# Attention and feed-forward on one core: row halves that exchange two banks, and weighing in 64-row pieces

## What is computed

```python
xn = _layernorm(x, axis=-1)                       # 4 x 2048 x 256
# attention: q, k, v = xn @ W + b, 16 heads of 16, q and k with rotary positions
scores = jnp.einsum('bhnd,bhmd->bhnm', q, k) / jnp.sqrt(jnp.float32(d))
weights = jax.nn.softmax(scores, axis=-1)
inter = jnp.einsum('bhnm,bhmd->bhnd', weights, v)
attn = inter.transpose(0, 2, 1, 3).reshape(b, n, d) @ Wo + bo
# feed-forward: w = where(k, 1, -1)
h = s0 * (concatenate([xn, -xn]) @ w0)            # 512 -> 1024
h = relu(h) * 2;  h = s1 * (h @ w1);  h = relu(h) * 2   # 1024 -> 1024
y = x + attn + s2 * (h @ w2)                      # 1024 -> 256
```

## Time and profile before

| | us |
|---|---|
| median of 3 runs | 2763.39 |
| lowest and highest run | 2763.38, 2764.12 |
| the profiled execution | 2764.13 |
| its span in the profile | 2762.3 |
| PE busy | 2670.4 (97%) |
| ScalarE (ACT) busy | 2099.4 (76%) |
| VectorE (DVE) busy | 957.2 (35%) |
| GpSimd (POOL) busy | 301.8 (11%) |

### The profile page before, as it was taken

One profiled execution on the slowest core, in us unless ns is written; L12 is line 12 of the kernel. 1 busy time (PEld: TensorE's weight loads), 2 busy tenths in 40 slices (PEclk: granted clock), 3 DMA queues, 4 the chain that ended last, 5 costly groups with the idle time before them and its releaser, 6 DMA issues.

```text
span 2762.3 us, 49767 instructions
## 1 busy us (share of the span) xinstructions
PE 2670.4 (97%) x21063; PEld 1416.9 (51%) x21063; DVE 957.2 (35%) x1535; ACT 2099.4 (76%) x2301; POOL 301.8 (11%) x265
## 2 busy tenths in 40 slices
PE   7999499999999999999999999999999999999997
PEld 6777245454444445454545454544545454545444
DVE  6776222323232323242332333232423223232322
ACT  4556388888888887878787878788887878787883
POOL 4666100000000000000000000000000000000000
PEclk9999699999999999999999999999999999999998
DMA  8888412212222222122121222221222222222213
GB/s 252 256 260 251 109 40 55 55 51 55 59 59 59 74 54 72 52 71 69 48 71 55 70 66 74 57 78 50 75 57 59 64 60 67 60 74 66 73 25 111
DMA packets 288417, 228.67 MB, mean 83 GB/s; under 512 B 184129, under 2 KB 227905, under 8 KB 281665
## 3 DMA queue, kind: packets, MB, share of 16 engines
q1 hardware_dynamic: 279744, 217.08, 28.6%
q10 hardware_dynamic: 8448, 8.39, 0.9%
HBM read 140.46 MB, written 84.93 MB: 82 GB/s over the span
## 4 chain that ended last, share of the span: by engine, by line
PE 80%; ACT 5%; issue 2%; SPq 1%; DMA 1%; DVE 0%; POOLq 0%; POOL 0%; DVEq 0%
PE ps_o L946 33%; PE ps_f L981 23%; PE ps_s L931 21%; ACT probs L911 5%; PE ps_f L994 2%; PE ps_f L1036 0%; SPq L826 0%; DMA xT_lo<-xn_lo_d 0%; DMA probs<-rest_sum_d 0%; PE ps_o L1036 0%; DVE k_rows L1141 0%; SPq L823 0%; DMA heads_t<-heads 0%; SPq L728 0%; POOLq L740 0%
## 5 line engine op out<-in xcount | busy, mean ns | idle before, releaser
L911 ACT ACTIVATE probs<-ps_s 128x1024 f32<-128x1024 f32 x2048 | 1945.5, 1032 | 480.1 <-PE ps_s L931 469.4
L946 PE MATMUL ps_o<-probs,v_ones 128*32 128x512 f32 x8192 | 1011.3, 600 | 0.0
L931 PE MATMUL ps_s<-q_rows,k_rows 50*128 50x512 f32 x4096 | 858.7, 440 | 35.6 <-DMA q_rows<-row_shift 31.0
L931 PEld LDWEIGHTS ps_s<-q_rows,k_rows 50*128 50x128 f32 x4096 | 366.8, 184 | 688.0 <-ACT probs L911 600.7
L1110 DVE TENSOR_SCALAR h_hi<-ps_f 128x512 fp32r<-128x512 f32 x224 | 154.4, 689 | 921.5 <-PE ps_f L981 921.4
L946 PEld LDWEIGHTS ps_o<-probs,v_ones 128*32 128x32 f32 x8192 | 200.6, 108 | 426.6 <-issue 331.0
L981 PE MATMUL ps_f<-h_hi,ffn_w 64*128 64x512 f32 x2048 | 409.7, 395 | 0.0
L981 PE MATMUL ps_f<-h_lo,ffn_w 64*128 64x512 f32 x2048 | 405.2, 390 | 0.0
L1055 POOL TENSOR_TENSOR heads<-heads,sums 128x512 f32<-128x512 f32 x64 | 82.5, 1289 | 2166.9 <-DVE sums L1076 2166.9
L1076 DVE RECIPROCAL sums<-sums 128x128 f32<-128x128 f32 x256 | 228.4, 925 | 1.1
L981 PEld LDWEIGHTS ps_f<-h_hi,ffn_w 64*128 64x128 f32 x2048 | 196.3, 186 | 37.3 <-issue 10.1
(11 more groups left out here) (102 smaller groups left out, 1611.9 us busy)
## 6 DMA issues: line engine op xcount, KB each, us to landing
k_rows<-k_parts SPq DMA_DIRECT2D x128, 256.0 KB
q_rows<-q_parts SPq DMA_DIRECT2D x384, 64.0 KB
q_parts<-parts SPq DMA_DIRECT2D x32, 512.0 KB, 3.7
k_parts<-parts SPq DMA_DIRECT2D x32, 512.0 KB, 5.5
k_rows<-k_parts SPq DMA_DIRECT2D x128, 128.0 KB
x_chunk<-in_x ACTq DMA_DIRECT2D x16, 512.0 KB, 6.1
xn_hi_d<-xn_hi SPq DMA_DIRECT2D x16, 512.0 KB, 4.4
xn_lo_d<-xn_lo SPq DMA_DIRECT2D x16, 512.0 KB, 5.2
```

Of the source, the lines that this page charges most:

```text
L911: nc.scalar.activation(probs[:, s % PBUF, half * 2 * C:(half + 1) * 2 * C], ps_s[:, half].rearrange("p c n -> p (c n)"), ACT.Exp, scale=SC ...
L931: last = nc.tensor.matmul(ps_s[:, half, w], k_rows[rows, u, t * P:(t + 1) * P], q_rows[rows, u, half], start=True, stop=True)
L946: last = nc.tensor.matmul(ps_o[32 * c:32 * c + 2 * DH], v_ones[:, u, t], probs[:, s % PBUF, c * C:(c + 1) * C], start=(t == 0), stop=(t == ...
```

## The change

The feed-forward work goes in groups of two outputs with two stages. In stage 0 the upper row half adds to bank 0 and the lower to bank 1; in stage 1 they change banks (`bank = half ^ stage`), so that both halves of a sum meet in the bank itself. ps_f has two banks instead of three, and ps_o two instead of one. VectorE copies a finished group's two banks to raw, and makes hi and lo from there. carry goes. The third layer is one group: a bank holds two outputs of 256 columns.

Weighing issues, for each step, eight matmuls of 64 rows by 32 columns: four with the upper 64 keys into one bank of ps_o, four with the lower into the other. `finish` copies one bank and adds the other.

The parts are spread evenly: VISITS_PER_ROUND gives the three visits of a round 4, 2, 2 parts in the first layer, 3, 3, 2 in the second and 6, 5, 5 in the third, hence 4, 16 and 4 rounds. Before it is 4, 15 and 5. The projection moves from round 31 to 39, the pass's last, and SP's store of y to the end of the pass.

```diff
-BANKS = 3
+GROUPS = (FT // 2, FT // 2, 1)
-PROJECT_AT = 3 * len(BURSTS) + 1
+PROJECT_AT = 4 * len(BURSTS) - 1
+VISITS_PER_ROUND = ((4, 2, 2), (3, 3, 2), (6, 5, 5))
+K_LAST = FT - 2
+def stage_parts(layer):
+    if layer < THIRD:
+        return [(0, k, low) for k in range((DT, FT)[layer]) for low in range(2)]
+    return [(t, k, low) for ks in (range(K_LAST), range(K_LAST, FT)) for t in range(TT // 2) for k in ks for low in range(2)]
...
-        carry = sb("carry", [P, 2, C], F32)
+        raw = sb("raw", [P, 2, C], F32)
-        ps_o = ctx.enter_context(nc.psum_tensor("ps_o", [P, C], F32))
-        ps_f = ctx.enter_context(nc.psum_tensor("ps_f", [P, BANKS, C], F32))
+        ps_o = ctx.enter_context(nc.psum_tensor("ps_o", [P, 2, C], F32))
+        ps_f = ctx.enter_context(nc.psum_tensor("ps_f", [P, 2, C], F32))
...
-                sp.wait_ge(group_used, outs_before(i, projects) + OUTS[projects] + BANKS)
+                sp.wait_ge(group_used, 2 * number_of(i + 1, FIRST, 0))
+                if projects:
+                    sp.sem_inc(turn_begun, 1)
+                    sp.dma_start(y_out[b - 1, r], y[:]).then_inc(y_stored, 16)
                 sp.sem_inc(turn_begun, 1)
                 sp.dma_start(rest_out[b, r], rest[:]).then_inc(rest_stored, 16)
                 store_head(i, HEADS - 1)
...
-                for c in range(CB):
-                    last = nc.tensor.matmul(ps_o[32 * c:32 * c + 2 * DH], v_ones[:, u, t], probs[:, s % PBUF, c * C:(c + 1) * C],
-                                            start=(t == 0), stop=(t == KT - 1))
+                for half in range(2):
+                    rows = slice(GROUP_ROWS * half, GROUP_ROWS * (half + 1))
+                    for c in range(CB):
+                        last = nc.tensor.matmul(ps_o[32 * c:32 * c + 2 * DH, half], v_ones[rows, u, t],
+                                                probs[rows, s % PBUF, c * C:(c + 1) * C], start=(t == 0), stop=(t == KT - 1))
...
+                if first and stage == 1:
+                    pe.wait_ge(stage_done, number - max(0, i - CB) + 1)
+                if first and stage == 0:
...
+                    if number > 0:
+                        pe.wait_ge(group_used, 2 * number - 1)
...
                 for half in range(2):
+                    if half == 1 and first and stage == 0 and number > 0:
+                        pe.wait_ge(group_used, 2 * number)
                     rows = slice(GROUP_ROWS * half, GROUP_ROWS * (half + 1))
+                    bank = half ^ stage
...
+                number = number_of(i, THIRD, 1)
                 pe.wait_ge(y_loaded, 32 * i - 32 * (CB - 1))
                 for t in range(TT):
+                    half, n = t // 2, t % 2
+                    if n == 0:
+                        pe.wait_ge(group_used, 2 * number - 1 + half)
...
-                nc.vector.tensor_copy(heads[:, u], ps_o[:]).then_inc(raw_ready, 1)
+                nc.vector.tensor_copy(heads[:, u], ps_o[:, 0]).then_inc(half_kept, 1)
+                dve.wait_ge(half_kept, HEADS * i + j + 1)
+                nc.vector.tensor_tensor(heads[:, u], heads[:, u], ps_o[:, 1], ALU.add).then_inc(raw_ready, 1)
...
+                for bank in range(2):
+                    nc.vector.tensor_copy(raw[:, bank], ps_f[:, bank]).then_inc(group_used, 1)
...
             def take_projected(i):
...
-                for t in range(TT):
-                    at = PROJECT_PLACE + t
-                    dve.wait_ge(group_done, outs_before(i, True) + at + 1)
-                    nc.vector.tensor_tensor(y[:, t], ps_f[:, at % BANKS, 0:D], y[:, t], ALU.add).then_inc(group_used, 1)
+                dve.wait_ge(group_done, number_of(i, THIRD, 1) + 1)
+                for half in range(2):
+                    pair = y[:, TT // 2 * half:TT // 2 * (half + 1)].rearrange("p t d -> p (t d)")
+                    nc.vector.tensor_tensor(pair, ps_f[:, half], pair, ALU.add).then_inc(group_used, 1)
...
+                    for layer, group in ENDS[n]:
+                        take(i, layer, group)
                     if ended % KT == 0:
                         finish(i, j)
```

More of the change, by code:

```diff
@@ L105, in rounds @@
         out.append(left[:n])
-        ends.append([(layer, phase) for visit in left[:n] for layer, phase, part in visit if part == size_of(layer) - 1])
+        ends.append([(layer, group) for visit in left[:n] for layer, group, stage, *part in visit
+                     if stage == 1 and last_of(layer, stage, tuple(part))])
         left = left[n:]
@@ L979, in beside @@
-                    begins = part == 0 and (half == 0 or phase == 0)
-                    ends = part == size - 1 and (half == 1 or phase == sums_in(layer) - 1)
-                    last = nc.tensor.matmul(to, lhs, rhs, start=begins, stop=ends)
-                    if ends:
-                        last.then_inc(group_done, 1)
-                    elif part == size - 1:
-                        last.then_inc(half_done, 1)
+                    bank = half ^ stage
+                    if layer == THIRD:
+                        out = TT // 2 * bank + t
+                        to, lhs, rhs = ps_f[:, bank, t * D:(t + 1) * D], (h2_hi, h2_lo)[low][rows, k, out * P:(out + 1) * P], w2[rows, k]
+                    else:
+                        out = 2 * group + bank
+                        to, on = ps_f[:, bank], slice(out * P, (out + 1) * P)
+                        lhs = (w0, w1)[layer][rows, k, on]
+                        rhs = ((xT_hi, xT_lo), (h1_hi, h1_lo))[layer][low][rows, k]
@@ L1006, in one_pass @@
                         if 0 <= visit < len(VISITS[n]):
[L1007 to L1008 removed]
+                            for part in VISITS[n][visit]:
+                                beside(i, *part)
                     if projects and n == PROJECT_AT:
@@ L1076, in invert, with take @@
                 nc.vector.reciprocal(at, at).then_inc(sums_inverted, 1)
-            def keep(i, projects, layer):
-                bank = ps_f[:, place(projects, layer, 0) % BANKS]
-                dve.wait_ge(group_done, outs_before(i, projects) + place(projects, layer, 0) + 1)
+            def take(i, layer, group):
+                number = number_of(i, layer, group)
+                done = SUMS * i + FT * layer + 2 * group
+                dve.wait_ge(group_done, number + 1)
                 if layer == THIRD:
@@ new lines, in take @@
+                    for bank in range(2):
+                        to = rest[:, TT // 2 * bank:TT // 2 * (bank + 1)].rearrange("p t d -> p (t d)")
+                        nc.vector.scalar_tensor_tensor(out=to, in0=ps_f[:, bank], scalar=w["scale"][:, 0:1], in1=to,
+                                                       op0=ALU.mult, op1=ALU.add).then_inc(group_used, 1)
+                    return
+                if done > 0:
+                    dve.wait_ge(part_ready, done)
+                for bank in range(2):
+                    nc.vector.tensor_copy(raw[:, bank], ps_f[:, bank]).then_inc(group_used, 1)
```

143 lines of the change are left out of this document (47 added, 96 removed).

## The result

| | us |
|---|---|
| changed kernel, median of 4 runs | 2811.73 |
| lowest and highest run | 2809.08, 2812.81 |
| kernel before, median of 4 runs | 2763.39 |
| ratio, 95% interval | 1.0174, 1.0156 to 1.0191 |
| the profiled execution, its span | 2812.81, 2811.0 |

The change makes the kernel 48 us slower. The forecast was 20 us slower.

What follows compares the result with a forecast made beforehand. PE, at 97% of the span, was taken as the bound. Terms of -32.6, +2.0, +38.5, +2.0 and +10.4 gave +20.3 us on a span of 2762.3, so 2784 us as median, range 2762 to 2813.

Steps and rivals of the forecast that it cites:

- visits, 16 passes: Feed-forward rounds in each pass: evenly spread parts save 2.04 us a pass, -32.6 us; first-layer rounds taken at 4.97.
- pieces of 64 rows, 16 passes: Weighing: eight pieces side by side start the last one 0.027 us later in each two-step round, +10.4 us.
- projecting passes, 12: Round after the projection: 12 projecting passes lose the 0.17 us they had from an idle ScalarE, +2.0 us.
- wait at the boundary, 11: Start of the pass after passes 4 to 14: first feed-forward pair waits 3.5 us for VectorE's y adds, +38.5 us.
- half clock at it, 11: Pass boundaries: rival that PE's idle 2.6 us lowers the clock, +28 us, 2812; 12%, not in the sum.
- end: Last pass: the additional add and the y adds stand before the final reciprocals, +2.0 us, up to +5.
- The rival that it is hidden: Pass boundary: the next pass's first part does not wait for VectorE, so the time is 2746; 4%.
- the rival in series: Weighing: the eight pieces do not run together, each round ends 0.43 us later, +275 us, 3059; 8%.
- That ScalarE covers it in one-step rounds: Weighing in one-step rounds: ScalarE's 0.14 us covers the 0.027 us delay, so only two-step rounds count it.
- VectorE's: VectorE's added copies and adds: some 200 us more busy time on an engine at 35%, priced 0.
- The switch: Change between scores and weighing: columns still change, so the 0.10 us pause stays, 0 us; rival of a free switch, 2653, 7%.

Runs made afterwards that it cites:

- kernel 5: Changed kernel with VectorE adding the projection into y before finishing head 3, and weighing in 128 rows by 32 columns without VectorE's add: 2743.04 us.
- kernel 2: Changed kernel with 13 extra score pairs, results overwritten, issued by PE before the wait at the start of passes that follow a projecting one: 2790.86 us.
- kernel 4: Kernel before with only its feed-forward visits spread evenly (16 second-layer and 4 third-layer rounds) and the projection one round later: 2757.43 us.
- Kernel 1: Changed kernel with two VectorE calls exchanged: in a pass's last round it adds the projection into y before finishing head 3, not after: 2754.72 us.
- kernels 6 and 7: Changed kernel, y additions before head 3's end, weighing one query chunk in 128 columns: two 64-row pieces, 2617.16 us, or one 128-row piece, 2768.02 us.
- kernel 3: Changed kernel with weighing as before, four matmuls of 128 rows by 32 columns into one bank, and VectorE's copy without the add: 2786.73 us.

## Why the prediction was off

The terms beside what the runs measure, in us:

```
term                                  forecast   measured   from
visits, 16 passes                      -32.6      -25.9     147.37 -> 145.75 (kernel 5)
pieces of 64 rows, 16 passes           +10.4      +10.2     145.75 -> 146.39 (kernel 5, changed)
projecting passes, 12                   +2.0       +2.5     +3.45 -> +3.66 on a pass
wait at the boundary, 11               +38.5      +39.4     5.085 -> 8.67 (kernel 2)
half clock at it, 11                     0        +20.4     8.67 -> 10.53 (changed)
end                                     +2.0       +1.4     pass 15 to the end, 186.0 -> 192.1, less the above
sum                                    +20.3      +48.0     span +48.7
```

**The step that failed is the clock.** The prediction had the wait right, in place and in size, and listed what could follow from it: PE with some 2.6 us of nothing, and then the 1.2 GHz level, 11 x 2.5 = 28 us, 2812 in all. It gave that 12% and put zero into the sum. Measured are 20.4 us in the first rounds and 20.9 between the medians of the changed kernel and kernel 2, and the time is 2811.7. That 2812 is nearly the measured time is partly luck: the 28 us were too many, and the visits gave 7 less than said. The only row on the clock was of a far longer idle time, so the trace of before couldn't decide it. Yet the same trace has no idle stretch of PE above 0.07 us between 340 and 2700 us, so a clock of 1.00 there was no evidence that PE can idle for almost 3 us and keep it. The fault was to treat the absence of such a case as a reason for the high level.

**The visits** gain 0.42 us less in a pass than said. First-layer rounds take 5.06 to 5.08 with 128 rows, not 4.97, and 4 x 0.10 = 0.40 of the 0.42 is that. The prediction counted one exposed load in such a round, the one at the swap; the rows above show the second, for which the last scores wait for ScalarE. The second layer's rounds came out as said (4.88, 4.99), and kernel 4 confirms that the spread alone gives most of it.

**The boundary** was right nearly to the digit: the second y addition starts 3.04 us after the first scores (forecast 3.03), and the wait is 3.59 (3.5). The rival that it is hidden falls. Kernel 1 shows what the prediction didn't ask: the wait isn't in the new banks but in the order of two calls on VectorE.

**The weighing** was right: the eight pieces run together (the rival in series falls), and a two-step round after another is 0.026 longer (0.027). That ScalarE covers it in one-step rounds was wrong: the 16 of a pass are 0.024 longer each. The 16 two-step rounds that follow a one-step round are the covered ones: in the second layer they take 4.994 and 4.999, where 0.027 was counted for each. As there are 16 of either kind, the two errors cancel, and that the pass came out right (0.64 and 0.65) is luck.

**VectorE's** larger share of the work cost nothing, as said, but its size was off: busy time grew by 74 us (957.2 to 1031.1), not by some 200. Part of that is that h_hi, made from raw in SBUF, takes 0.42 us (L1085) where it took 0.69 from PSUM (L1110 before).

**The switch** was right: 0 in the changed kernel. The prediction's reason, that the columns still change, is shown by kernels 6 and 7: rows alone don't matter as long as columns differ, and the other way round.

What stays open is what sets the moment at which the clock falls, and why a fall inside the wait brings 6.8 us at half clock (6 of 6) and one behind it 3.4 (16 of 16, in the changed kernel and kernel 3).

## What to carry to other kernels

When PE gets a new wait of 2 or 3 us, price it twice: the wait itself, and PE at the 1.2 GHz level for some us behind it (here 3.59 and 1.86 us at each place), unless the trace holds a wait of that size with the clock kept. Before changing the buffers, look at what the engine that must free them does first: here two calls exchanged on VectorE, which isn't the bound, were worth 57 us. The change of the array's shape was paid in full here as long as rows or columns differed, so making one of them equal bought nothing.

## What the runs showed of the hardware

- The granted clock fell to half at each of 11 idle times of PE of 2.77 to 3.13 us, and at each of 11 of 2.01 us (kernel 3); it stayed at 1.00 over 12 of 0.66 us (kernel 4), and when the long wait was filled with matmuls whose results are thrown away (kernel 2), by which the kernel became 21 us faster.
- A fall before PE went on was followed by 6.8 us at half clock, one after it by 3.4, in all 22 cases. The long stretch cost 2.3 us, the short one 1.3.
- The pause at a switch of shape is the same 0.10 us for a change of rows, of columns and of both, and is gone (0.002 or 0.003 us from start to load) only when both agree (kernels 6 and 7).
- Eight fp32 pieces of 64 rows by 32 columns run side by side; the four added ones lengthen a two-step round after another by 0.026 us, a one-step round by 0.024, and one that ScalarE holds up by 0.005 (changed kernel).
- VectorE makes a 512-wide h_hi in 0.42 us from SBUF and in 0.69 from PSUM (changed kernel and before).
